# Attention values as 64x64 matmuls without empty columns, and all rounds written out, in a three-attention transformer layer

## The chip, the cores and the metric

The kernel runs on one core of a Trainium2 chip. The metric is the device time of one execution in microseconds. Before the change it is 1069.2 us, the median of three runs (1064.68 to 1073.83). The core has TensorE (PE; its weight loads are PEld), VectorE (DVE), ScalarE (ACT), GpSimd (POOL) and the DMA queue of SyncE (SP). Each runs its own stream of instructions and they wait for each other on semaphores. All data is fp32.

## What is computed

64 sequences of 64 tokens with 256 features go through self-attention (A), cross-attention (B), an MLP (M), and a second cross-attention (C), each with 16 heads of 16 features:

```python
def attention(q, k, v, mask):
    scores = jnp.einsum('bhqd,bhkd->bhqk', q, k) / jnp.sqrt(jnp.float32(HD))
    scores = scores * mask - 10000.0 * (1.0 - mask)
    probs = jax.nn.softmax(scores, axis=-1)
    return jnp.einsum('bhqk,bhkd->bhqd', probs, v)

x = x + merge(attention(A's q, k, v of layernorm(x))) @ w_ao + b_ao
x = x + merge(attention(B's q of layernorm(x); k, v of ctx)) @ w_co + b_co
x = x + gelu(layernorm(x) @ w1 + b1) @ w2 + b2
y = x + tanh(gate) * merge(attention(C's q of x; k, v of layernorm(ctx))) @ Wo.T
```

## The kernel before

**Tiling.** A unit is 4 sequences (256 tokens) as T = 2 tiles of 128 rows; a tile holds TILE = 2 sequences of 64 tokens. There are U = 16 units. Round i works on five units at once: P (load and first statistics) on unit i, A on i-1, B on i-2, M on i-3 and C on i-4. So there are rounds 1 to 19 for TensorE, of which the first and last few work on fewer stages. Rounds 5 to 15 run as a hardware loop (`Fori`, function `run`), the others are written out. Within a round the order of each engine is that of its `body`, written by hand; TensorE's goes: `turn` of C.xT and B.cT, C.K and C.Q, `turn` of M.zT and A.zT, B.V, B.zT, scores C, B.K, B.Q, M.H0, M.H1, scores B, M.H2, attend C, A.K, A.Q, A.V, M.H3, C.OT, M.cT, scores A, C.AO, attend B, M.Y0, B.OT, M.V (values of C for the next round), attend A, B.AO, A.OT, M.Y1, A.AO.

**Banks.** PSUM has 8 banks: `s_bank0` to `s_bank3` for everything of attention, `pj0` to `pj3` for the projections, given out in turn (table PJ); `claim` waits until a bank's last use was read. M.H0 claims the bank that B.V was in, so it waits for `value_rows` of B.

**Attention.** 16 heads are 8 pairs. Bank r = 2t + half holds tile t and 4 pairs. Scores (L482) use 64 rows of the array at a time, the two halves by turns. VectorE masks them into `prob` (`mask_scores`, L847), GpSimd adds the offset (not for C), VectorE takes row maxima (`row_max`, L852), GpSimd subtracts them (L1089), ScalarE takes exp (L692). Then `turn_probs` (L493) transposes each 128x128 block back into the same bank and ScalarE copies it to `prob` (`turned_back`, L698). `values` (L504), for each quarter r, has 4 matmuls with a 128x128 block of transposed probabilities as the stationary operand (the weights: 128 rows are 2 sequences x 64 keys, 128 columns the 64 queries of the pair's two heads) and `vz` as the moving one: 66 columns, for each sequence b2 the 32 values of the pair and a one. In `vz` the rows of the other sequence are zero, so that the sequences stay apart: every column is half empty, and of the results each half of the partitions uses only its own head's 16 of 32 columns. The column of ones gives the sum of the probabilities.

**Reading.** `value_rows` (L841) copies the projection of V into `vz`, by tile and sequence, 4 copies of 64 partitions x 256 elements. `normalise` (L861, L866) takes, for each quarter r, the reciprocal of the sums and multiplies, once for each half of the partitions: 3 instructions, 12 in a unit. `turn_out` (L521) transposes `o` once all quarters are normalised; ScalarE and VectorE make the high and low part of it (`oT_hi` L651, `oT_lo` L828), and the output projection (C.AO and so on, L446) reads both.

An fp32 matmul of the program appears in the trace as two records of MATMUL and two of LDWEIGHTS; a transpose or an fp32r one (the projections) as one of each.

## Time and profile before

| | |
|---|---|
| median of the runs | 1069.2 us |
| span of the profiled execution | 1072.6 us |
| TensorE, weight loads | 967.9 us (90%), 929.0 us (87%) |
| VectorE | 866.5 us (81%) |
| ScalarE, GpSimd | 576.3 us (54%), 561.3 us (52%) |
| mean granted TensorE clock | 0.947 of 2.4 GHz |

Busy time counts an engine's instructions from start to end; matmuls overlap, so a busy TensorE is not one at its peak. The profiled execution is 3.4 us above the median of the runs. Times in rows are microseconds from the start of the span, durations of one instruction nanoseconds where the form says so.

### The profile page before, as it was taken

What the parts mean: (1) busy time and instruction counts of PE and PEld (TensorE: products, weight loads), DVE (VectorE), ACT (ScalarE), POOL (GpSimd) and SP (SyncE); (2) the same over time, 40 slices, a digit from 0 to 9 for tenths busy, and PEclk for the clock granted to TensorE, in tenths of its full rate; (3) what the DMA queues carried; (4) which work ended last, traced back from release to release, by engine and by line L of the source; (5) the groups of instructions that cost most, each with busy time, mean ns of one, the idle gap of its engine ahead of it and who ended that gap; (6) DMA issues with size and microseconds to landing.
All of it is one profiled execution on the core that took longest, in us unless ns stands there. A gap on an engine that the chain in (4) does not pass through costs nothing.

```text
span 1072.6 us, 23111 instructions
## 1 busy us (share of the span) xinstructions
PE 967.9 (90%) x8336; PEld 929.0 (87%) x8336; DVE 866.5 (81%) x1946; ACT 576.3 (54%) x1109; POOL 561.3 (52%) x566
## 2 busy tenths in 40 slices
PE   6977799999999998999999898999999899998876
PEld 6866798989989998988999898998999899998875
DVE  6586979888897978889797988889797888778553
ACT  3444646565474556646464656547455664646342
POOL 2254647457283746638274745728474563727221
PEclk9589999998999899999989999899989999898995
DMA  5030100101000010101001010100101010000000
GB/s 192 0 96 1 36 1 12 37 11 36 11 10 26 9 35 10 35 10 35 10 0 35 10 35 10 35 10 0 35 10 35 10 36 1 26 13 7 17 10 10
DMA packets 32936, 25.74 MB, mean 24 GB/s; under 512 B 12672, under 2 KB 32000, under 8 KB 32896
## 3 DMA queue, kind: packets, MB, share of 16 engines
q1 hardware_dynamic: 32896, 25.20, 7.9%
q8 instruction: 26, 0.43, 0.2%
q14 instruction: 14, 0.11, 0.0%
HBM read 20.99 MB, written 4.19 MB: 23 GB/s over the span
## 4 chain that ended last, share of the span: by engine, by line
PE 44%; DVE 32%; issue 11%; POOL 6%; ACT 6%; DVEq 1%; DMA 0%; ACTq 0%; POOLq 0%; SPq 0%
PE s_bank L504 12%; PE pj L446 10%; PE s_bank L493 7%; PE pj L431 6%; DVE o L866 5%; PE pj L460 4%; DVE rmax_A L852 3%; POOL prob_AC L1089 2%; DVE prob_AC L847 2%; DVE stats L892 2%; DVE z_A L906 2%; PE pj L521 2%; DVE rmax_C L852 2%; PE s_bank L482 2%; DVE z_B L906 2%
## 5 line engine op out<-in xcount | busy, mean ns | idle before, releaser
L683 ACT ACTIVATE k<-pj,kbias,consts 128x256 f32<-128x256 f32 x192 | 92.7, 564 | 143.1 <-PE pj L431 143.1
L1065 POOL TENSOR_TENSOR veps<-mv,eps 128x2 f32<-128x2 f32 x64 | 15.6, 243 | 263.2 <-DVE mv L898 263.2
L1089 POOL TENSOR_TENSOR prob_AC<-prob_AC,rmax_C 128x512 f32<-128x512 f32 x64 | 65.6, 1054 | 125.4 <-DVE rmax_C L852 125.4
L692 ACT ACTIVATE prob_AC<-prob_AC 128x512 f32<-128x512 f32 x128 | 81.1, 636 | 89.5 <-POOL prob_AC L1089 89.4
L1096 POOL TENSOR_TENSOR h_lo<-g,h_hi 128x512 fp32r<-128x512 f32 x64 | 81.4, 1292 | 47.3 <-DVE h_hi L1051 47.3
L482 PE MATMUL s_bank<-k,q 64*128 64x128 f32 x1536 | 100.3, 281 | 6.3 <-ACT q L670 3.8
L482 PEld LDWEIGHTS s_bank<-k,q 64*128 64x128 f32 x1536 | 91.0, 191 | 14.2 <-issue 4.7
L504 PE MATMUL s_bank<-vz_C,prob_AC 128*128 128x66 f32 x512 | 74.7, 316 | 16.5 <-ACT prob_AC L698 16.5
L504 PEld LDWEIGHTS s_bank<-vz_C,prob_AC 128*128 128x128 f32 x512 | 72.7, 231 | 19.5 <-issue 19.4
L1080 POOL TENSOR_TENSOR prob_AC<-prob_AC,maskA_off 128x512 f32<-128x512 f32 x64 | 79.9, 1284 | 17.2 <-DVE prob_AC L847 17.2
L1080 POOL TENSOR_TENSOR prob_B<-prob_B,maskB_off 128x512 f32<-128x512 f32 x64 | 83.0, 1329 | 10.7 <-DVE prob_B L847 10.6
L651 ACT ACTIVATE oT_hi<-pj,bias 128x256 fp32r<-128x256 f32 x96 | 40.0, 470 | 89.2 <-PE pj L521 89.2
L431 PE MATMUL pj<-zT_M_hi,w_hi_M 128*128 128x256 f32 x256 | 75.6, 296 | 6.9 <-DVE vz_B L841 6.9
L698 ACT ACTIVATE prob_AC<-s_bank 128x512 f32<-128x512 f32 x128 | 66.7, 621 | 14.1 <-PE s_bank L493 14.1
L460 PE MATMUL pj<-w_hi_M,h_hi 128*128 128x256 f32 x256 | 74.1, 289 | 0.0
L493 PE MATMUL s_bank<-consts,prob_AC 128*128 128x128 f32 x512 | 67.5, 287 | 6.4 <-ACT prob_AC L692 3.3
L431 PE MATMUL pj<-zT_M_lo,w_hi_M 128*128 128x256 f32 x256 | 72.8, 284 | 0.0
L431 PE MATMUL pj<-zT_M_hi,w_lo_M 128*128 128x256 f32 x256 | 72.7, 284 | 0.0
L460 PE MATMUL pj<-w_lo_M,h_hi 128*128 128x256 f32 x256 | 71.6, 280 | 0.0
L460 PE MATMUL pj<-w_hi_M,h_lo 128*128 128x256 f32 x256 | 71.5, 279 | 0.0
L493 PEld LDWEIGHTS s_bank<-consts,prob_AC 128*128 128x128 f32 x512 | 60.4, 148 | 8.9 <-issue 5.4
L1089 POOL TENSOR_TENSOR prob_AC<-prob_AC,rmax_A 128x512 f32<-128x512 f32 x64 | 65.6, 1049 | 4.2 <-DVE rmax_A L852 3.6
(199 smaller groups left out, 3324.7 us busy)
## 6 DMA issues: line engine op xcount, KB each, us to landing
x_in<-in_x SPq DMA_DIRECT2D x16, 256.0 KB, 2.7
ctx_b<-in_ctx SPq DMA_DIRECT2D x16, 256.0 KB, 2.9
ctx_c<-in_ctx SPq DMA_DIRECT2D x16, 256.0 KB, 2.8
out<-y SPq DMA_DIRECT2D x16, 256.0 KB, 2.2
g<-in_w_M SPq DMA_DIRECT2D x2, 1024.0 KB, 7.1
maskB<-in_mask_Bx1xSxS_ff SPq DMA_DIRECT2D x32, 64.0 KB, 2.6
prob_AC<-in_w_A_qkv SPq DMA_DIRECT2D x1, 768.0 KB, 4.5
prob_B<-in_w_B_kv SPq DMA_DIRECT2D x1, 512.0 KB, 6.1
```

The source lines that it names most:

```text
L431: last = nc.tensor.matmul(bank[:, m * TOK:(m + 1) * TOK], wt[:, k, col + m * P:col + (m + 1) * P], x[:, k, :], start=(n == 0), stop=(n == ...
L446: last = nc.tensor.matmul(bank[:, t * H:(t + 1) * H], x[:, k, t * P:(t + 1) * P], wt[:, k, col:col + H], start=(n == 0), stop=(n == 3 * KC ...
L460: last = nc.tensor.matmul(bank[:, 0:H], x[:, k, t * P:(t + 1) * P], wt[:, k, :], start=(n == 0), stop=(n == 3 * (FF // P) - 1))
L482: mm = nc.tensor.matmul(bank[:, c, :, b2, :], q2[rows_, c, t * TILE + b2].rearrange("p e q -> p (e q)"), k2[rows_, c, t * TILE + b2], star ...
L493: last = nc.tensor.transpose(s_bank[r][:, n * P:(n + 1) * P], prob[a][:, r, n, :], ident[:, :])
L504: last = nc.tensor.matmul(s_bank[r][:, n * TILE * VW:(n + 1) * TILE * VW], prob[a][:, r, n, :], vz[a][:, t, half * BL + n, :, :], start=Tr ...
L683: last = nc.scalar.activation(k2[:, m, :, s, :], k_all[:, m], ACT.Identity, bias=kbias[:, "ABC".index(a), s, m:m + 1], scale=parity[:, 2 + ...
L692: nc.scalar.activation(p2, p2, ACT.Exp).then_inc(exped[a], 1)
L698: nc.scalar.activation(prob[a][:, r, :, :].rearrange("p n k -> p (n k)"), s_bank[r][:, :], ACT.Copy).then_inc(turned_in[a], 1)
L1080: nc.gpsimd.tensor_tensor(p3, p3, of_tile(maskA_off if a == "A" else maskB_off, a, r), ALU.add).then_inc(offset[a], 1)
L1089: nc.gpsimd.tensor_tensor(p3, p3, rmax[a][:, r, :].unsqueeze(2).broadcast_to([P, BL * TILE, S]), ALU.subtract).then_inc(shifted[a], 1)
L1096: nc.gpsimd.tensor_tensor(h_lo[:, 2 * m:2 * m + 2, :], g[:, m, :, :], h_hi[:, 2 * m:2 * m + 2, :].bitcast(F32), ALU.subtract).then_inc(h_l ...
```

## The change

`values` works on squares of 64x64 of the array. For each tile t, pair m, head e of the pair and sequence b2 there is one matmul: the weights are the 64 rows of b2 and the 64 columns of e of the same transposed block, the moving operand is 16 value columns and the one, and the result goes to the partitions of e in bank 2t + b2, columns 17m to 17m + 16. `vz` has no zeros any more (VW is 17), and the results have no unused columns. A unit has 64 matmuls where it had 16. Values of a tile start when both its quarters are turned back, as they write to both banks of the tile. `value_rows` is one copy, `normalise` two instructions for each of two tiles, and the banks are waited for by tile. The four banks are one tensor. `run` writes out all rounds. One more wait (`const_in`) stands ahead of each tile's values; it is long fulfilled.

```diff
-VW = 2 * HD + 1
+VW = HD + 1
...
-            for i in range(first, min(FIRST, last + 1)):
-                body(i)
-            with eng.Fori(FIRST, U) as i:
-                body(i)
-            for i in range(U, last + 1):
+            for i in range(first, last + 1):
                 body(i)
...
-                    read = masked if b[0][0] == "S" else normed
-                    pe.wait_ge(read[b[0][2]], R * (b[1] - 1) + r + 1)
+                    if b[0][0] == "S":
+                        pe.wait_ge(masked[b[0][2]], R * (b[1] - 1) + r + 1)
+                    else:
+                        pe.wait_ge(normed[b[0][2]], T * (b[1] - 1) + r // HALVES + 1)
...
-                pe.wait_ge(turned_in[a], R * u + r + 1)
-                t, half = divmod(r, HALVES)
-                for n in range(BL):
-                    last = nc.tensor.matmul(s_bank[r][:, n * TILE * VW:(n + 1) * TILE * VW],
-                                            prob[a][:, r, n, :], vz[a][:, t, half * BL + n, :, :],
-                                            start=True, stop=True)
-                last.then_inc(summed[a], 1)
+                pe.wait_ge(turned_in[a], R * u + HALVES * (t + 1))
+                pe.wait_ge(const_in, 16)
+                for m in range(NPAIR):
+                    half, n = divmod(m, BL)
+                    for e in range(2):
+                        for b2 in range(TILE):
+                            rows_ = slice(b2 * S, (b2 + 1) * S)
+                            mm = nc.tensor.matmul(
+                                s_banks[e * S:(e + 1) * S, t * HALVES + b2, m * VW:(m + 1) * VW],
+                                prob[a][rows_, t * HALVES + half, n, e * S:(e + 1) * S],
+                                vz[a][rows_, t, e, m, :], start=True, stop=True)
+                            if (m, e) == (NPAIR - 1, 1):
+                                mm.then_inc(summed[a], 1)
...
-                for t in range(T):
-                    for b2 in range(TILE):
-                        rows_ = slice(b2 * S, (b2 + 1) * S)
-                        dst = vz[a][rows_, t, :, b2, 0:2 * HD].rearrange("p m (e f) -> p m e f", e=2)
-                        last = nc.vector.tensor_copy(dst, v[rows_, t])
-                last.then_inc(pj_free[pj_bank(name)], 1)
+                dst = vz[a][:, :, :, :, :].rearrange("p t e m v -> p (t e m) v")[:, :, 0:HD]
+                nc.vector.tensor_copy(dst, pj[pj_bank(name)][:, :].rearrange("p (n f) -> p n f", f=HD)).then_inc(
+                    pj_free[pj_bank(name)], 1)
...
-                for r in rs:
-                    dve.wait_ge(summed[a], R * u + r + 1)
...
+                for t in ts:
+                    dve.wait_ge(summed[a], TILE * (T * u + t + 1))
+                    sums = s_banks[:, t * HALVES:(t + 1) * HALVES, 0:NPAIR * VW].rearrange(
+                        "p b (m v) -> p b m v", v=VW)
+                    nc.vector.reciprocal(rden[a][:, t, :, :], sums[:, :, :, HD]).then_inc(inverted[a], 1)
+                    dve.wait_ge(inverted[a], T * u + t + 1)
+                    nc.vector.tensor_tensor(
+                        o[:, t * TILE:(t + 1) * TILE, :, :], sums[:, :, :, 0:HD],
+                        rden[a][:, t, :, :].unsqueeze(3).broadcast_to([P, TILE, NPAIR, HD]),
+                        ALU.mult).then_inc(normed[a], 1)
...
-                    if active("B", i):
-                        normalise("B", i, [r])
+                    if active("B", i) and r % HALVES == 0:
+                        normalise("B", i, [r // HALVES])
```

TensorE in attend C of a written-out round, before: the transposes of the fourth quarter, then values (each row is followed by what it waits for):

```order
L493 MATMUL s_bank<-consts,prob_AC 128x128 [waits exped_C,masked_B]
L493 MATMUL s_bank<-consts,prob_AC 128x128 x3
L504 MATMUL s_bank<-vz_C,prob_AC 128x66 [waits turned_in_C,pj_free2]
L504 MATMUL s_bank<-vz_C,prob_AC 128x66 x3
L504 MATMUL s_bank<-vz_C,prob_AC 128x66 [waits turned_in_C]
L504 MATMUL s_bank<-vz_C,prob_AC 128x66 x3
```

and the same place after:

```order
L469 MATMUL s_bank<-consts,prob_AC 128x128 [waits exped_C,masked_B]
L469 MATMUL s_bank<-consts,prob_AC 128x128 x3
L485 MATMUL s_bank<-vz_C,prob_AC 64x17 [waits const_in,turned_in_C,pj_free2]
L485 MATMUL s_bank<-vz_C,prob_AC 64x17 x31
L485 MATMUL s_bank<-vz_C,prob_AC 64x17 [waits const_in,turned_in_C]
L485 MATMUL s_bank<-vz_C,prob_AC 64x17 x31
```

Four groups of 4 matmuls, one for each quarter, have become two of 32, one for each tile.

VectorE from `normalise` of C to the low part of C.OT, before (of the four quarters the last):

```order
L861 RECIPROCAL rden_C<-s_bank 128x8 [waits summed_C]
L866 TENSOR_TENSOR o<-s_bank,rden_C 64x2x64 [waits inverted_C]
L866 TENSOR_TENSOR o<-s_bank,rden_C 64x2x64
L841 COPY vz_A<-pj 64x8x32 [waits pj_full3]
L841 COPY vz_A<-pj 64x8x32 x3
L1051 CAST h_hi<-g 128x512 [waits pj_free0,pj_full1]
L828 SCALAR_TENSOR_TENSOR oT_lo<-pj,bias,oT_hi 128x256 [waits hi_C_OT]
```

and after, all of it:

```order
L836 RECIPROCAL rden_C<-s_bank 128x16 [waits summed_C]
L838 TENSOR_TENSOR o<-s_bank,rden_C 128x256 [waits inverted_C]
L836 RECIPROCAL rden_C<-s_bank 128x16 [waits summed_C]
L838 TENSOR_TENSOR o<-s_bank,rden_C 128x256 [waits inverted_C]
L876 TENSOR_SCALAR z_A<-x_in,mv,rstd 128x256 [waits ln_rstd_A]
L876 TENSOR_SCALAR z_A<-x_in,mv,rstd 128x256
L815 COPY vz_A<-pj 128x32x16 [waits pj_full3]
L1021 CAST h_hi<-g 128x512 [waits pj_free0,pj_full1]
L806 SCALAR_TENSOR_TENSOR oT_lo<-pj,bias,oT_hi 128x256 [waits hi_C_OT]
```

Of the 16 instructions for `rden_C`, `o` and `vz_A` that stood ahead of the low part of C.OT, 5 are left; the rest of VectorE's order is the same.

## Rows read from the trace of the kernel before

**Rows 1.** Page: the span, and each engine's busy time, share and instructions.

```profile
span 1072.6 us, 23111 instructions
PE 967.9 (90%) x8336; PEld 929.0 (87%) x8336; DVE 866.5 (81%) x1946; ACT 576.3 (54%) x1109; POOL 561.3 (52%) x566
```

**Rows 2.** Timeline of TensorE, first transposes of five rounds: start, duration (us), instruction.

```profile
156.40 0.60 PE L415 MATMUL pj<-consts,x 128*128 128x128 f32 x4
...
216.89 0.49 PE L415 MATMUL pj<-consts,x 128*128 128x128 f32 x3
...
462.99 0.60 PE L415 MATMUL pj<-consts,x 128*128 128x128 f32 x4
...
523.59 0.60 PE L415 MATMUL pj<-consts,x 128*128 128x128 f32 x4
...
586.06 0.60 PE L415 MATMUL pj<-consts,x 128*128 128x128 f32 x4
```

**Rows 3.** Waits: who waited for whom; us in total, times, longest.

```profile
POOL prob_AC L1089 <- DVE rmax_C L852: 125.4, 18, 17.6
ACT prob_AC L692 <- POOL prob_AC L1089: 89.4, 110, 8.0
...
PE pj L415 <- DVE z_B L906: 20.2, 15, 2.6
...
PE pj L446 <- DVE oT_lo L828: 16.7, 12, 2.4
PE s_bank L504 <- ACT prob_AC L698: 16.5, 14, 1.2
...
PEld pj L521 <- DVE o L866: 8.9, 16, 3.1
...
PE pj L431 <- DVE vz_B L841: 6.9, 14, 0.5
```

**Rows 4.** Stretches: from:to, length; busy (x) by engine; clock, DMA share, GB/s.

```profile
27.10:31.00 3.90, 3.90 (x21) 3.90 (x20) 2.06 (x3) 0.33 (x1) 3.90 (x5) 0.50 0.00 0
35.50:41.70 6.20, 6.20 (x32) 6.20 (x30) 2.35 (x9) 5.07 (x8) 0.00 (x0) 0.50 0.00 0
549.30:556.00 6.70, 6.70 (x33) 6.70 (x33) 6.38 (x17) 1.11 (x3) 6.70 (x8) 0.50 0.00 0
566.00:569.50 3.50, 3.50 (x34) 3.50 (x32) 2.94 (x8) 1.28 (x3) 3.50 (x5) 1.00 0.54 152
```

**Rows 5.** Line L394: durations (ns) min/median/max, first and last start (us), shapes.

```profile
L394 PE MATMUL pj<-consts,prob_B x8: 250/250/272, 24.7 to 25.5; 128*128 128x1 f32 x8
```

**Rows 6.** Timeline of TensorE: start of values B; transposes, scores A, C.AO.

```profile
503.55 0.67 PE L504 MATMUL s_bank<-vz_B,prob_B 128*128 128x66 f32 x5
...
560.01 0.60 PE L415 MATMUL pj<-consts,ctx_c 128*128 128x128 f32 x4
560.54 2.06 PE L482 MATMUL s_bank<-k,q 64*128 64x128 f32 x32
562.53 0.39 PE L446 MATMUL pj<-w_hi_C_o,oT_hi 128*128 128x256 f32 x1
562.75 0.28 PE L446 MATMUL pj<-w_hi_C_o,oT_lo 128*128 128x256 f32 x1
```

**Rows 7.** Timeline of ScalarE: exp of B, and its four turned-back quarters.

```profile
499.44 2.20 ACT L692 ACTIVATE prob_B<-prob_B 128x512 f32<-128x512 f32 x4
502.30 2.06 ACT L698 ACTIVATE prob_B<-s_bank 128x512 f32<-128x512 f32 x4 [0.66 <-PE s_bank L493]
```

**Rows 8.** Groups by line: shapes, count, busy us, mean ns, idle before.

```profile
L847 DVE TENSOR_TENSOR prob_B<-s_bank,maskB 128x512 f32<-128x512 f32 x64 | 39.9, 685 | 2.4 <-PE s_bank L482 2.0
...
L866 DVE TENSOR_TENSOR o<-s_bank,rden_B 64x128 f32<-64x128 f32 x128 | 36.9, 289 | 3.1
...
L841 DVE COPY vz_B<-pj 64x256 f32<-64x256 f32 x64 | 26.8, 419 | 0.6
...
L861 DVE RECIPROCAL rden_B<-s_bank 128x8 f32<-128x8 f32 x64 | 13.3, 208 | 11.0 <-PE s_bank L504 9.0
```

More of the change, by code:

```diff
@@ L194, in build @@
         k2 = sb("k2", [P, KC, UB, 2, S])
-        vz = {a: sb(f"vz_{a}", [P, T, NPAIR, TILE, VW]) for a in "ABC"}
+        vz = {a: sb(f"vz_{a}", [P, T, 2, NPAIR, VW]) for a in "ABC"}
         prob = {"B": sb("prob_B", [P, R, BL, TILE * S]),
@@ L201, in build @@
         rmax = {a: sb(f"rmax_{a}", [P, R, BL * TILE]) for a in "ABC"}
-        rden = {a: sb(f"rden_{a}", [P, R, BL * TILE]) for a in "ABC"}
+        rden = {a: sb(f"rden_{a}", [P, T, TILE, NPAIR]) for a in "ABC"}
         o = sb("o", [P, UB, NPAIR, HD])
@@ L207, in build @@
         h_lo = sb("h_lo", [P, FF // P, TOK], F32R)
-        s_bank = [ps(f"s_bank{r}") for r in range(R)]
+        s_banks = ctx.enter_context(nc.psum_tensor("s_bank", [P, R, BANK], F32))
+        s_bank = [s_banks[:, r, :] for r in range(R)]
         pj = [ps(f"pj{n}") for n in range(PJ_BANKS)]
@@ L479, in scores @@
                                 rows_ = slice(half * S, (half + 1) * S)
-                                bank = s_bank[t * HALVES + half][:, :].rearrange(
+                                bank = s_bank[t * HALVES + half].rearrange(
                                     "p (c s b k) -> p c s b k", c=KC, s=2, b=TILE)
@@ L511, in attend @@
                     turn_probs(a, r, i)
-                for r in range(R):
-                    values(a, r, i)
+                for t in range(T):
+                    values(a, t, i)
             def turn_out(a, i):
                 name = f"{a}.OT"
-                pe.wait_ge(normed[a], R * (unit(a, i) + 1))
+                pe.wait_ge(normed[a], T * (unit(a, i) + 1))
                 bank = claim(name, i)
@@ L772, in _ @@
             for a in "ABC":
-                last = nc.vector.memset(vz[a][:, :, :, :, :], 0.0)
-            last.then_inc(zeroed, 1)
-            dve.wait_ge(zeroed, 1)
-            for a in "ABC":
-                for b2 in range(TILE):
-                    last = nc.vector.memset(vz[a][b2 * S:(b2 + 1) * S, :, :, b2, 2 * HD:VW], 1.0)
+                last = nc.vector.memset(vz[a][:, :, :, :, HD:VW], 1.0)
             last.then_inc(ones_set, 1)
@@ L835, in value_rows @@
                 dve.wait_ge(pj_full[pj_bank(name)], pj_use(name, i))
-                v = pj[pj_bank(name)][:, :].rearrange("p (t e m f) -> p t m e f", t=T, e=2, m=NPAIR)
-                for t in range(T):
-                    for b2 in range(TILE):
-                        rows_ = slice(b2 * S, (b2 + 1) * S)
-                        dst = vz[a][rows_, t, :, b2, 0:2 * HD].rearrange("p m (e f) -> p m e f", e=2)
-                        last = nc.vector.tensor_copy(dst, v[rows_, t])
-                last.then_inc(pj_free[pj_bank(name)], 1)
+                dst = vz[a][:, :, :, :, :].rearrange("p t e m v -> p (t e m) v")[:, :, 0:HD]
+                nc.vector.tensor_copy(dst, pj[pj_bank(name)][:, :].rearrange("p (n f) -> p n f", f=HD)).then_inc(
+                    pj_free[pj_bank(name)], 1)
             def mask_scores(a, r, i):
@@ L853, in row_max, with normalise @@
                                         AX.X, ALU.max).then_inc(maxed[a], 1)
-            def normalise(a, i, rs=range(R)):
+            def normalise(a, i, ts=range(T)):
                 u = unit(a, i)
-                for r in rs:
-                    dve.wait_ge(summed[a], R * u + r + 1)
-                    t, half = divmod(r, HALVES)
-                    sums = s_bank[r][:, 0:BL * TILE * VW].rearrange("p (n v) -> p n v", v=VW)
-                    nc.vector.reciprocal(rden[a][:, r, :], sums[:, :, 2 * HD]).then_inc(inverted[a], 1)
-                    dve.wait_ge(inverted[a], R * u + r + 1)
-                    for e in range(2):
-                        rows_ = slice(e * S, (e + 1) * S)
-                        last = nc.vector.tensor_tensor(
-                            o[rows_, t * TILE:(t + 1) * TILE, half * BL:(half + 1) * BL, :],
-                            sums[rows_, :, e * HD:(e + 1) * HD].rearrange("p (n b) f -> p b n f", b=TILE),
-                            rden[a][rows_, r, :].rearrange("p (n b) -> p b n", b=TILE).unsqueeze(3).broadcast_to(
-                                [S, TILE, BL, HD]), ALU.mult)
-                    last.then_inc(normed[a], 1)
+                for t in ts:
[8 more added lines that the diff above has]
+                        ALU.mult).then_inc(normed[a], 1)
             def tokens_out(stage, bank_use, dst, residual, i):
```

6 lines of the change are left out of this document (3 added, 3 removed).

## The prediction

> **What bounds the kernel now.** The page comes first: TensorE is busy for 90% of the span and its weight loads for 87%, VectorE for 81%, ScalarE and GpSimd for about half [rows 1]. So TensorE carries the time, with VectorE close behind. Next the timeline of TensorE: the start of each round is the first transpose of L415. A straight round took 216.89 - 156.40 = 60.49 us, two rounds of the loop 60.60 and 62.47 us [rows 2]. The view of waits tells what stands in TensorE's way [rows 3]: each round it waits for `z_B` (20.2 us in 15 waits, 1.3 us each), for `vz_B` (0.5 us), for the first turned-back probabilities of C (16.5 in 14, 1.2 us) and, in about every second round, for `oT_lo` (16.7 in 12, 1.4 us); its weight loads wait for `o` (8.9 us in 16; without the longest, 0.4 us each). The table of stretches shows why rounds differ: from 549.3 to 556.0 us, in the values of C that follow that 1.2 us wait and in A.K behind them, the granted clock was 0.5 (1.2 of 2.4 GHz) [rows 4]. A round with this dip is 1.9 us longer; the work lost is more, up to half of these 6.7 us, some 3.1 us, since such a round swallows the wait for `oT_lo` of C.
>
> **The change: the values matmuls.** Now a unit of one attention has 16 matmuls in the program, which the trace shows as 32 pairs of weight load and matmul; they run at 3.5 us for 32 [rows 4], 0.11 us a pair. After, it has 64, so 128 pairs, each with 64 weight columns and 17 moving columns instead of 128 and 66. What sets the pace? The setup matmuls of L394 move a single column against 128 weight columns, and 8 of them start within 0.8 us [rows 5]: again 0.11 us. So the weight columns set it. I take half the columns as half the time, 0.055 us a pair (an estimate; nothing here loads 64 columns). Then how many squares run at once? Scores work on two halves of the array's rows, 128 weight columns each: 32 pairs from 560.54 to 562.53 us, 1.99 us, of which 0.2 is taken off below: 0.056 us a pair [rows 6]: two at a time. The squares differ in row half from one to the next too. Bounds for the 128 pairs:
> - all four squares at once: 128 x 0.055 / 4 = 1.8 us;
> - two at a time: 128 x 0.055 / 2 = 3.5 us;
> - no better than a pair of scores: 128 x 0.056 = 7.2 us.
>
> I take two at a time, which is what the nearest row shows, and 3.5 us, no different from today.
>
> [...] No run here has such small squares.
>
> **Entering and leaving the squares.** Around the scores TensorE loses time: the last of four transposes (560.01 us, 0.11 us apart) would hand over at 560.45, scores start at 560.54; their 16 double steps of 0.11 us would end at 562.32, C.AO starts at 562.53, and its second matmul comes 0.22 us after the first instead of 0.12 [rows 6]. That is 0.4 us for in and out. Values have no such cost now and get it three times a round; in C the way in lies under a wait. [...] So values cost +0.4 us each: +0.3 in C, +0.4 in B and A, **+1.1 us a round**.
>
> **Coarser wait.** Values now start after two turned-back quarters, not one. ScalarE turns them back 0.52 us apart (4 in 2.06 us) [rows 7]. In C, where TensorE waits for the first, this costs 0.5 us. In B the second is back at 502.30 + 1.03 = 503.33, and values start at 503.55 today [rows 6, 7]: hidden, with 0.2 us to spare. If that cover is gone, 0.2 to 0.5 us each. A is alike.
>
> **VectorE.** `value_rows`: 4 copies of 64x256 at 0.42 = 1.68 us become one of 128x512 from PSUM; the like-sized L847 takes 0.69, so -1.0 us. `normalise`: 4 x (0.21 + 2 x 0.29) = 3.15 us become 2 x (0.21 + a 128x256 multiply). That multiply lies between 0.29 and 0.69; I take 0.45: 1.3 us, so -1.85 [rows 8]. Per round -8.5 us of VectorE's work. It is worth only what TensorE waits for:
> - `vz_B` copied 1.0 us sooner ends the 0.5 us wait before M.H0. Behind it row maxima of C, GpSimd's shift, ScalarE's exp and the turning back also come 1.0 us sooner (each waits for the one before, [rows 3]); less the 0.5 for the second quarter, values of C start **0.5 us** sooner. The M.H0 gain is contained in that, as TensorE waits again in C.
> - `oT_lo` of C: VectorE reaches it 2.85 us sooner (normalise C, copy of `vz_A`). In a round without the dip its wait, some 1.3 us, goes; the dipped round has none to lose. But ScalarE's exp of B then bounds: its activations end at 501.6, the turning back begins at 502.3 [rows 7], and TensorE, which came to values of B at 503.55 [rows 6], can gain little more than what exp itself starts sooner by; I keep half, **-0.7**.
> - `o` before B.OT: **-0.3** in all rounds, as `normalise` of B ends sooner.
>
> **Straight code.** Straight and looped rounds differ by 0.1 us [rows 2]: **-0.1**. TensorE's instruction stream grows by half (8336 to some 12,900 matmuls); that it flows 128 pairs in 3.5 us, 27 ns a pair, is not shown by a row. The scores' 56 ns is the nearest, and 7.2 us the bound above.
>
> **Sum.** Round without dip: 1.1 - 0.5 - 0.7 - 0.3 - 0.1 = -0.5. With dip: +0.2. Some 13 full rounds, half and half: about -2 us. The three filling and three draining rounds wait on chains through VectorE: the waits for `o` beyond the steady ones and sooner `vz` are worth 0.5 to 1 us a round, about -4. From its own span of 1072.6 us: 1066.6. The profiled execution is 3.4 us above the median of 1069.2, so in the median's terms **1063 us**.
>
> **Rivals.**
> - *Four squares at once.* For it: scores start their two halves together, so the array runs tiles apart. Against: nothing shows two column halves in the same rows. 1.8 us instead of 3.5, thrice a round, is -5.1; TensorE would then stand longer for exp and z_B, so I keep two thirds, -3.4 x 13 = -44, with the other rounds -50: 1013 us.
> - *The clock.* With one moving column per load the granted clock was 0.5 (27.1 to 31.0 us), and it stayed there through dense values of A (35.5 to 41.7 us), while values of B at full clock kept it [rows 4]. Squares move 17 columns at a time, side by side. If values of B or of A cost a dip in each round and C in each instead of half, that is 13 x 3.1 + 6 x 1.9 = +52; if both B and A do, +92. With 1063: 1115 to 1155. [...] This is the slower side: it decides once one further dip a round appears.
> - *Squares hardly overlap, or the stream of instructions limits.* At 0.04 us a pair, 5.1 us: +1.6 x 48 = +77, 1140; at the bound, +178, 1240.
> - *Faster VectorE buys nothing*: then +1.1 x 16 less 4, 1077, within the same forecast.
>
> **Chances.** Two at a time without further dips 0.35 (own range 1050 to 1078); four at once or close to it 0.27; the clock 0.2; slow squares 0.18. A difference of 1% is about what a measurement can tell. Faster by over 1% (below 1058.5): 0.27 and a third of 0.35 less what the clock eats, 0.37; within 1%: 0.24; slower: 0.39. The range of 1005 to 1130 leaves out the fastest of the second case and the slow tails, each about 0.1.
>
> **What would show it.** The rows of values: 128 pairs in 3.5 us (right), under 2.5 (four at once), over 5 (slow). Granted clock in values of B and A: 1.00, or 0.50. The start of C.AO no longer waiting for `oT_lo`. `normalise` of C in 1.3 us instead of 3.2. VectorE's busy time near 866 - 8.5 x 16 = 730 us. The forecast is wrong above all if 64 weight columns don't load in half the time of 128, or if the column halves of the array run apart.

## The result and the profile after

The changed kernel takes 1011.4 us (median; 999.65 to 1023.91), the kernel before 1069.2 us: a ratio of 0.9395, 95% interval 0.9346 to 0.9445, so 6% faster. The forecast was 1063 us, no change. The profiled execution is the slowest of its runs, 1023.9 us; places and pauses below are read from it, sizes from runs.

The page of the kernel after, answering to [rows 1], with the instruction queues' rows and the shares of the chain that ended last:

```profile
span 1022.1 us, 30512 instructions
PE 913.7 (89%) x12944; PEld 867.1 (85%) x12944; DVE 722.3 (71%) x1412; ACT 571.3 (56%) x1109; POOL 561.7 (55%) x566
...
q8 instruction: 104, 1.70, 0.7%
...
PE 74%; DVE 12%; issue 6%; ACT 4%; POOL 3%; DMA 0%; SPq 0%; DVEq 0%; ACTq 0%; POOLq 0%
```

VectorE has lost 144 us of busy time (forecast: 730 us left). TensorE is the bound. The queue q8, which brings instructions, moved 104 packets of 16 KB; before it was 26.

TensorE in one round with no stop inside values (start, duration, instruction, in brackets the idle time), answering to [rows 2] and [rows 6]:

```profile
738.62 0.60 PE L389 MATMUL pj<-consts,x 128*128 128x128 f32 x4
...
746.04 0.66 PE L389 MATMUL pj<-consts,z_B 128*128 128x128 f32 x4 [0.75 <-DVE z_B L876]
...
761.22 2.06 PE L485 MATMUL s_bank<-vz_C,prob_AC 64*64 64x17 f32 x128 [1.22 <-issue]
763.21 0.38 PE L405 MATMUL pj<-zT_A_hi,w_hi_A_qkv 128*128 128x256 f32 x1
...
772.19 0.39 PE L420 MATMUL pj<-w_hi_C_o,oT_hi 128*128 128x256 f32 x1
772.41 0.28 PE L420 MATMUL pj<-w_hi_C_o,oT_lo 128*128 128x256 f32 x1
...
775.86 2.06 PE L485 MATMUL s_bank<-vz_B,prob_B 64*64 64x17 f32 x128
777.84 0.39 PE L434 MATMUL pj<-w_hi_M,h_hi 128*128 128x256 f32 x1
778.07 0.28 PE L434 MATMUL pj<-w_hi_M,h_lo 128*128 128x256 f32 x1
...
788.52 0.38 PE L420 MATMUL pj<-w_hi_B_o,oT_lo 128*128 128x256 f32 x1 [0.53 <-issue]
...
793.87 0.60 PE L389 MATMUL pj<-consts,x 128*128 128x128 f32 x4
```

The round takes 793.87 - 738.62 = 55.25 us, where it was 60.5. Each values takes 1.98 us from its first square to the next operation (761.22 to 763.21, 775.86 to 777.84), where it was 3.5: three times 1.5 is 4.5 of the 5.2 us. The stand at 788.52, behind values of A, is not in the shortest rounds of this trace: the one from 324.61 us takes 54.42. C.AO no longer waits for `oT_lo`. Values of C still stand 1.2 us, now for the second turned-back quarter.

But only some rounds are like that. TensorE in values of A at 425 us of the same kernel:

```profile
425.31 1.82 PE L485 MATMUL s_bank<-vz_A,prob_AC 64*64 64x17 f32 x111 [0.35 <-issue]
429.09 0.43 PE L485 MATMUL s_bank<-vz_A,prob_AC 64*64 64x17 f32 x17 [1.96 <-issue]
429.44 0.47 PE L420 MATMUL pj<-w_hi_B_o,oT_hi 128*128 128x256 f32 x1
429.71 0.42 PE L420 MATMUL pj<-w_hi_B_o,oT_lo 128*128 128x256 f32 x1
429.93 0.42 PE L420 MATMUL pj<-w_lo_B_o,oT_hi 128*128 128x256 f32 x1
```

After 111 of 128 pairs TensorE stands still for 2 us, with nothing to wait for, and then goes on at half the clock (a matmul of 256 columns every 0.22 us instead of 0.12). The table of stretches (from:to, length; busy time and count of PE, PEld, DVE, ACT, POOL; granted clock; DMA) has it, with the half clock behind the same at 476 us and the round from 738.6 us below:

```profile
427.20:429.10 1.90, 0.01 (x3) 0.01 (x2) 0.03 (x1) 0.00 (x0) 0.00 (x0) 1.00 0.00 0
429.40:432.70 3.30, 3.30 (x23) 3.27 (x18) 0.98 (x3) 0.00 (x0) 0.00 (x0) 0.53 0.03 5
...
479.00:484.10 5.10, 5.10 (x28) 5.08 (x24) 1.28 (x3) 1.89 (x3) 2.07 (x3) 0.50 0.28 73
738.60:793.80 55.20, 52.03 (x806) 49.48 (x805) 44.39 (x86) 34.47 (x68) 34.96 (x36) 1.00 0.09 24
```

This happens in 11 of the 48 values, 1.4 to 2.4 us each, 22 us together. Four more stands of this kind lie behind values, among other matmuls: 2.8 us long at 718.7, 0.8 at 787.7, 1.5 at 818.7 and 1.2 at 837.7 us. The waits of the kernel after, answering to [rows 3] (us in total, times, longest):

```profile
PE s_bank L485 <- issue: 41.6, 39, 2.1
...
PE pj L389 <- DVE z_B L876: 13.2, 15, 2.6
...
PE pj L420 <- DVE oT_lo L806: 7.1, 5, 2.0
```

The wait for `oT_lo` fell from 16.7 to 7.1 us, that for `z_B` from 20.2 to 13.2, that for `vz_B` before M.H0 is gone. What stands in front of squares is now "issue", 41.6 us: the turned-back quarters of C in most rounds, and the stops.

VectorE's new instructions, by shape (ns: least, median, most), answering to [rows 8]:

```profile
L838 DVE TENSOR_TENSOR o<-s_bank,rden_B x32: 423/424/426, 77.3 to 944.1; 128x256 f32<-128x256 f32 x32
...
L836 DVE RECIPROCAL rden_B<-s_bank x32: 245/257/258, 77.0 to 943.8; 128x16 f32<-128x16 f32 x32
...
L815 DVE COPY vz_B<-pj x16: 678/680/681, 55.9 to 919.1; 128x512 f32<-128x512 f32 x16
```

### The profile page after: what moved, and what is told of

The parts are those of the page before. It is cut to its first block, busy times and chain, and to the rows that moved or that the text cites. A ratio compares the mean times of both kernels' runs of the same rounds, so it can differ in the third digit from the quotient of the medians.

```text
span 1022.1 us, 30512 instructions
## 1 busy us (share of the span) xinstructions
PE 913.7 (89%) x12944; PEld 867.1 (85%) x12944; DVE 722.3 (71%) x1412; ACT 571.3 (56%) x1109; POOL 561.7 (55%) x566
## 4 chain that ended last, share of the span: by engine, by line
PE 74%; DVE 12%; issue 6%; ACT 4%; POOL 3%; DMA 0%; SPq 0%; DVEq 0%; ACTq 0%; POOLq 0%
PE pj L405 20%; PE pj L420 13%; PE s_bank L485 10%; PE pj L434 10%; PE s_bank L469 9%; PE s_bank L458 7%; DVE z_B L876 4%; PE pj L389 2%; PE pj L504 2%; DVE stats L862 1%; POOL rstd L1037 1%; DVE h_hi L1021 1%; DVE oT_lo L806 1%; PE pj L368 1%; DVE xT_C_lo L801 1%
## 5 line engine op out<-in xcount | busy, mean ns | idle before, releaser
L675 ACT ACTIVATE prob_AC<-prob_AC 128x512 f32<-128x512 f32 x128 | 77.8, 643 | 75.4 <-POOL prob_AC L1059 75.4
L434 PE MATMUL pj<-w_hi_M,h_hi 128*128 128x256 f32 x256 | 80.2, 313 | 2.7 <-issue 2.7
L434 PE MATMUL pj<-w_hi_M,h_lo 128*128 128x256 f32 x256 | 76.7, 300 | 0.9 <-issue 0.9
L434 PE MATMUL pj<-w_lo_M,h_hi 128*128 128x256 f32 x256 | 76.6, 299 | 0.0
L806 DVE SCALAR_TENSOR_TENSOR oT_lo<-pj,bias,oT_hi 128x256 fp32r<-128x256 f32 x96 | 41.5, 473 | 35.9 <-ACT oT_hi L634 35.9
L1059 POOL TENSOR_TENSOR prob_B<-prob_B,rmax_B 128x512 f32<-128x512 f32 x64 | 66.7, 1071 | 0.0
```

What stands on the lines that cost most here:

```text
L434: last = nc.tensor.matmul(bank[:, 0:H], x[:, k, t * P:(t + 1) * P], wt[:, k, :], start=(n == 0), stop=(n == 3 * (FF // P) - 1))
L675: nc.scalar.activation(p2, p2, ACT.Exp).then_inc(exped[a], 1)
L1059: nc.gpsimd.tensor_tensor(p3, p3, rmax[a][:, r, :].unsqueeze(2).broadcast_to([P, BL * TILE, S]), ALU.subtract).then_inc(shifted[a], 1)
```

## Experiments: straight code or a loop

Theory at this point: four squares run at once, VectorE's shorter work lets TensorE use that, and TensorE's stops inside values come from its instruction stream. Rivals: the straight code brings the gain or makes the stops; VectorE alone brings the gain.

**The changed kernel again** (`after_again`), on one chip with `e1_loop`, `e2_before_straight` and `e6_vector_undone`.

> The changed kernel once more, for a second profile beside the other runs. Theory of the instruction stream (written-out rounds make TensorE fetch its program, and values of a tile pair use it up faster than it comes): in the profile values again stand still for 1.5 to 2.3 us in roughly 10 of 48 units, at multiples of 256 instructions of TensorE's stream, in sum some 20 us, and the time differs from run to run by 1 to 2%. Rival, that these stalls were an accident of one profiled execution: none or one or two here. Time 1000 to 1024 us under both.

1009.6 us, ratio 0.9435 (0.9386 to 0.9484). Ten of the eleven stops are there again, in the same rounds behind the same pair, 0.7 to 2.2 us each and 17 us together; the one of values of B at 476 us is not. So the place is fixed and the length is not.

**A loop again** (`e1_loop`): rounds 5 to 15 as a hardware loop in the changed kernel. For the long fulfilled wait ahead of each tile's values an increment of a semaphore of its own stands.

```diff
-            for i in range(first, last + 1):
+            for i in range(first, min(FIRST, last + 1)):
+                body(i)
+            with eng.Fori(FIRST, U) as i:
+                body(i)
+            for i in range(U, last + 1):
                 body(i)
```

> The changed kernel with rounds 5 to 15 as a hardware loop again, as before the change; a semaphore increment of TensorE stands in place of the wait for the constants ahead of each tile's values. Theory of the instruction stream: in the loop no pauses inside values, fewer dips of the granted clock, so 20 to 30 us less than the changed kernel: 980 to 990 us; the spread between runs falls to below 0.5%. Rival, straight code helps or costs nothing (a straight round was 0.1 us shorter before): same as the changed kernel within 0.5%, 1003 to 1015 us, with the pauses still there, as a loop body of over 1600 TensorE instructions has to be fetched as well.

1009.1 us, ratio 0.9388 (0.9355 to 0.9421): no difference to straight code, and not the 980 to 990 us of my theory. The stops inside values are gone from the loop, as the theory had it; only two are left, in the straight rounds ahead of it. In their place TensorE stands at each of the ten passages from one iteration to the next, for 2.2 to 2.7 us, 23.5 us together, as much as the stops took; behind eight of the ten the clock falls to half (timeline of TensorE, end of one round, start of the next):

```profile
609.86 0.28 PE L425 MATMUL pj<-w_lo_A_o,oT_hi 128*128 128x256 f32 x1
612.13 0.65 PE L394 MATMUL pj<-consts,x 128*128 128x128 f32 x4 [1.99 <-issue]
...
614.02 0.42 PE L410 MATMUL pj<-cT_C_hi,w_hi_C_k 128*128 128x256 f32 x1
```

Its q8 moved 129 packets, spread over the whole loop; in the kernel before there were 26, and none between 271 and 894 us, that is from the second iteration of its loop to the end of the last, and TensorE did not stand at the edge (0.12 us from start to start across it). So the round of the kernel before, 1032 records of TensorE's matmuls and loads, stayed loaded, and the new one, 1608, is fetched anew each time.

**The kernel before, straight** (`e2_before_straight`), the same edit the other way round.

> The kernel before with nothing changed but all rounds written out. Theory of the instruction stream: values with 32 pairs in 3.5 us use the stream 7 times more slowly than squares do, so no pauses inside values, and the time is that of before within 0.5%: 1064 to 1074 us. Rival, straight code is a gain of its own: 0.3 us or more a round in VectorE's chain behind the loop's edge, 1055 to 1065 us. Third: straight code stalls here too, then over 1080 us.

1069.6 us, ratio 0.9981 (0.9956 to 1.0006). Straight code by itself is worth nothing here, and its 68 packets of q8 come without a stop of TensorE.

## Experiments: how many squares run at once

The order of the 32 squares of a tile decides which neighbours there are. In the change, they differ in the row half (b2), then the column half (e). Each of the three kernels is `e1_loop` with the loops of `values` in another order; the work is the same. Each was run twice.

**Only row halves differ** (`e3_rows_apart`):

```diff
-                for m in range(NPAIR):
-                    half, n = divmod(m, BL)
-                    for e in range(2):
+                for e in range(2):
+                    for m in range(NPAIR):
+                        half, n = divmod(m, BL)
                         for b2 in range(TILE):
```

> The looped version with the 64 matmuls of values in another order: all of one column half of the array first, then the other, so that neighbours differ in row half alone. Theory, each square of the array works by itself and a pair takes 0.055 us on its square: two at a time, 128 pairs in 3.6 us instead of 1.85. If TensorE's 1.7 us in 48 values were all on the path, 1009 + 80 us; with VectorE's chain beside it some of that is hidden, 1035 to 1075 us. Rival, the pace is that of the instruction stream (14 ns a pair in any order): 1.85 us again and 1009 us.

**Only column halves differ** (`e4_cols_apart`): b2 outermost, then m, e innermost.

> As the one before, but neighbours differ in column half alone: all pairs of one row half first. Theory, squares are independent in both directions: 3.6 us for 128 pairs, as with rows apart, and the same time. [...]

**One square at a time** (`e5_one_square`): e and b2 outermost, m innermost.

> As before, with all 16 matmuls of a square behind each other, so that neighbours share both halves: theory of independent squares, one at a time, 128 pairs in 7.1 us (0.055 us each, half of the 0.11 us of 128 weight columns), in which only the few at the borders of the squares overlap. TensorE is then the bound by far: 1009 + 48 x 5.3 less what was hidden, 1200 to 1260 us. Rival, TensorE reorders over many instructions and still overlaps squares: below 5 us.

Values of one unit in the timelines of `e1_loop`, of `e3_rows_apart`, of `e4_cols_apart` and of `e5_one_square` (the last one partly at half clock):

```profile
634.79 2.14 PE L490 MATMUL s_bank<-vz_C,prob_AC 64*64 64x17 f32 x128 [1.17 <-issue]
```
```profile
574.49 3.31 PE L490 MATMUL s_bank<-vz_B,prob_B 64*64 64x17 f32 x128 [0.29 <-issue]
```
```profile
579.08 3.31 PE L490 MATMUL s_bank<-vz_B,prob_B 64*64 64x17 f32 x128 [0.29 <-issue]
```
```profile
540.98 8.06 PE L490 MATMUL s_bank<-vz_B,prob_B 64*64 64x17 f32 x128 [0.29 <-issue]
```

From first to last start at full clock: 1.93 us in the loop and 1.85 in straight code with all four squares, 3.10 with two row halves, 3.10 with two column halves, 6.17 with one. So 48 ns for a square alone, 24 with either neighbour, 14.5 with four: my estimate of 55 ns for 64 weight columns was near, but column halves run apart just as row halves do: squares of one row half and two column halves take half the time of squares one after the other, 3.10 us and 6.17.

The times: 1089.5 us (ratio 1.0148, 1.0067 to 1.0228), 1111.2 us (1.035, 1.0261 to 1.044), 1366.0 us (1.2723, 1.2625 to 1.2821), at a mean clock of 0.910, 0.883 and 0.813 where `e1_loop` has 0.933. All three kernels are slower than I expected: the paces came nearly as they should, the times did not. Two at a time costs 48 x 1.2 = 56 us more than four by the pace alone, and 80 in the kernel's time. The clock can make the rest: `e3_rows_apart` spends 198 us at half clock, `e1_loop` 137, which costs at most half of the difference, 30 us (an estimate). `e4_cols_apart` has the pace of `e3_rows_apart` and is 22 us slower, with 263 us at half clock; why its clock stays low for longer no run shows.

`e3_rows_apart` is nearly the world of my forecast, with VectorE's shorter work and two squares at a time, and it is not 1063 but 1089 us. Its ten loop edges take 25 us, which the forecast did not have; without them it would come to about 1064 (an estimate; no straight version of it was run).

## Experiments: what VectorE's shorter work is worth

**All taken back** (`e6_vector_undone`): `e1_loop` with 4 copies in `value_rows`, and 4 reciprocals and 8 multiplies of half the partitions in `normalise`.

```diff
-                    nc.vector.reciprocal(rden[a][:, t, :, :], sums[:, :, :, HD]).then_inc(inverted[a], 1)
...
+                    for b in range(TILE):
+                        nc.vector.reciprocal(rden[a][:, t, b, :], sums[:, b, :, HD]).then_inc(inverted[a], 1)
...
+                        for e in range(2):
+                            rows_ = slice(e * S, (e + 1) * S)
+                            last = nc.vector.tensor_tensor(
+                                o[rows_, t * TILE + b, :, :], sums[rows_, b, :, 0:HD],
```

> The looped version of the changed kernel with VectorE's savings taken back: value rows in 4 copies of 64 partitions, normalise with 4 reciprocals and 8 half-partition multiplies in a unit. Squares stay. Theory A, the gain is TensorE's (1.65 us less in each of 48 values): VectorE's 8.5 us a round are worth less than 1 us a round, so at most 15 us above the looped version. Theory B, VectorE shares the bound and the squares alone would have given little: 35 to 60 us above the looped version, since TensorE then waits for the low part of C, for o and for the copies in every round.

1091.0 us, ratio 1.0174 (1.0139 to 1.0209): the squares without VectorE's part, in a loop, are 17 us slower than the kernel before, and VectorE's part is worth 82 us on top of the squares, more than the 35 to 60 of theory B. It stands 22 us at its ten loop edges, which the kernel before does not; without them it would come to about 1069 (an estimate). So the squares alone are worth little, but that they lose is not shown. Its page, its chain, and one of its waits:

```profile
PE 918.6 (85%) x12944; PEld 869.9 (80%) x12944; DVE 864.5 (80%) x1940; ACT 576.6 (53%) x1109; POOL 562.3 (52%) x566
...
DVE 41%; PE 38%; issue 12%; ACT 4%; POOL 3%; DVEq 1%; DMA 0%; SPq 0%; ACTq 0%; POOLq 0%
```
```profile
PE pj L509 <- DVE o L849: 38.4, 32, 3.9
```

The chain that ended last runs more through VectorE than through TensorE (41% and 38%; with the short work, in `e1_loop`, 9% and 76%), and TensorE stands 1.2 us before two of three `turn_out`, for `o` (38.4 us in 32 times).

**Only normalise taken back** (`e11_normalise_undone`), **only B's copy** (`e12_copies_B`), **only A's and C's copies** (`e13_copies_AC`):

> The looped changed kernel with only normalise taken back to 4 reciprocals and 8 half-partition multiplies a unit; the copy of V's rows stays one instruction. With both taken back it was 1091.0, 81.9 us above the looped kernel's 1009.1. Theory (VectorE is the bound with squares, each us of its work counts): normalise is some 5.6 of 8.5 us a round, so +54 us, 1063 us, with VectorE busy some 810 us. Rival 1 (only what stands ahead of TensorE's wait for o counts, the copies are hidden): all of it, 1085 to 1091. Rival 2 (the sooner copies of V, which start the row maxima of C, carry most): under +30, below 1040 us.

> The looped changed kernel (1009.1 us), with only the copy of B's value rows taken back to 4 copies of 64 partitions. Theory (the place counts: this copy stands ahead of the row maxima of C, on the chain row maxima, GpSimd, exp, turned back, values of C, and ahead of M.H0): about 1 us later each round, and dips of the clock behind the longer wait: +15 to +25 us, 1024 to 1034. Rival (a share like every other us of VectorE's work, a third of the 44 us that all three copies cost on top of normalise): +8 to +15, 1017 to 1024.

> The looped changed kernel (1009.1 us), with only the copies of A's and C's value rows taken back to 4 copies each. Theory (the place counts): the copy of A stands ahead of the low part of C.OT, for which C.AO waits 0.4 us a round, the copy of C ahead of normalise of A, for which A.OT waits; each is partly hidden: +5 to +12 us, 1014 to 1021. Rival (a share of VectorE's work, two thirds of 44): +20 to +30, 1029 to 1039. If each of the two kernels costs nearly nothing and only together with the slower normalise the copies cost 44, the price lies in VectorE's sum and not in a place.

| taken back | time | more than `e1_loop` | VectorE busy |
|---|---|---|---|
| nothing (`e1_loop`) | 1009.1 | | 723.1 |
| copies of A and C | 1012.9 (ratio 0.9414, 0.9356 to 0.9472) | 3.8 | 754.3 |
| copy of B | 1021.3 (0.9527, 0.9497 to 0.9557) | 12.1 | 741.1 |
| normalise | 1046.8 (0.9763, 0.9723 to 0.9802) | 37.6 | 811.9 |
| all | 1091.0 | 81.9 | 864.5 |

Normalise alone costs 37.6 us for 89 of VectorE's time, between the 54 of my theory and the under 30 of its second rival: not each microsecond counts. The 3.8 us of the copies of A and C are not clear of the noise (the intervals of the ratios overlap). All three copies alone sum to 16 us, but on top of the long normalise they cost 44, for 53 us of VectorE's time. Both my rules for them fail: neither their place nor a fixed share gives 16 and 44. The reading that fits is that with a short `normalise` VectorE has slack that swallows most of a copy, and that where it has little left, most of a microsecond of its work is one of the kernel's.

## Experiments: the turned-back probabilities of C

In a clean round the longest wait left is that of values of C. ScalarE (timeline of the kernel after) does three gelus, six activations, ahead of turning back, while the first of the transposed probabilities already stand ready (the transposes run from 758.09 to 760.00 us):

```profile
757.85 2.30 ACT L693 ACTIVATE g<-pj,bias 128x256 f32<-128x256 f32 x6
760.00 2.09 ACT L681 ACTIVATE prob_AC<-s_bank 128x512 f32<-128x512 f32 x4
```

**Two gelus ahead, one behind** (`e7_back_sooner` on `e1_loop`, `e8_straight_back` on the changed kernel):

```diff
-                    for m in range(GELU - 1):
+                    for m in range(GELU - 2):
                         gelus(m, i)
                 if active("C", i):
...
                     turned_back("C", i)
+                if active("M", i):
+                    gelus(GELU - 2, i)
```

> The looped version with ScalarE turning back the probabilities of C ahead of its third gelu instead of behind it, since TensorE waits 1.5 us a round for the second quarter. Theory, this wait is on the path: values of C start 0.8 us sooner, 12 rounds or so, 5 to 10 us off: 1000 to 1004 us. Rival, the gelu is what VectorE waits for next (the high parts stand between the row maxima of B): no gain or a loss of 5 us.

> The changed kernel, straight code, with one edit: ScalarE turns the probabilities of C back ahead of the third gelu, as in the looped kernel where that gave 22 us (1009.1 to 986.5). Theory: the gain is the end of TensorE's 1.5 us wait in values of C and of clock dips behind it, so it comes in straight code too: 1009.6 - 22, about 988 us. The instruction stream of TensorE is unchanged, so its stops of 1.4 to 2.4 us inside values stay, 11 of them, about 20 us together. Rival: in straight code those stops and their dips dominate, and half of the gain is lost: about 1000 us.

986.5 us in the loop, ratio 0.9202 (0.9144 to 0.9259), and 996.1 in straight code, 0.9284 (0.9258 to 0.9311): 23 and 14 us less than their bases. I had expected 1000 to 1004 and 988, with 1000 as the rival's: the first gave more, the second less. The first is the fastest kernel of this study. About 0.7 us a round comes from the wait, the rest from the clock: values of C and then A.K and A.Q behind them in `e1_loop`, and the same in `e7_back_sooner` (table of stretches; the clock is the third column from the end):

```profile
634.79:636.87 2.08, 2.08 (x129) 2.05 (x129) 2.08 (x5) 0.88 (x2) 2.00 (x4) 1.00 0.00 0
636.87:641.32 4.45, 4.45 (x30) 4.45 (x25) 4.38 (x9) 1.85 (x4) 4.45 (x5) 0.62 0.01 4
```
```profile
561.55:563.62 2.07, 2.07 (x129) 2.04 (x129) 2.07 (x4) 1.60 (x4) 1.99 (x4) 1.00 0.03 8
563.62:566.59 2.97, 2.97 (x30) 2.97 (x25) 2.95 (x6) 1.24 (x3) 2.97 (x4) 1.00 0.00 0
```

The wait ahead of values is 1.4 us in the first and 0.7 in the second (first start after the last transpose). Behind the longer one the same 24 matmuls and the first of A.V take 4.45 us at a clock of 0.62, behind the shorter 2.97 at 1.00. That is 0.7 + 1.5 = 2.2 us in this round. But not each round of `e1_loop` is like that: the pause is 1.4 us in all eleven, and the clock falls behind it in six. Here is one where it does not, values of C and the stretch behind them:

```profile
750.63:752.70 2.07, 2.07 (x128) 2.04 (x128) 2.07 (x5) 0.88 (x2) 1.99 (x4) 1.00 0.03 8
752.70:755.70 3.00, 3.00 (x32) 3.00 (x26) 2.93 (x7) 1.26 (x3) 3.00 (x4) 1.00 0.00 0
```

Eleven times 0.7 and six times 1.5 are 17 us, and the eleven rounds take 631.4 us in `e1_loop` and 614.8 in `e7_back_sooner`, 16.6 less; the rest of the gain lies in the filling and draining rounds. Behind the pause of 0.7 us the clock stays in all eleven. In straight code the trace of `e8_straight_back` still has nine stops inside values, 18 us together. What becomes of the other 9 us between the two gains was not followed further.

## Experiments: where the stream of instructions stops

In the trace of the kernel after, each stop inside values lies at one position: if TensorE's recorded instructions are counted from the start, behind number 193 of every 256. 256 of them fill one 16 KB packet of q8 (26,660 instructions, 104 packets). A values has 256 records, so one boundary falls into each; TensorE stops only where the boundary falls late, behind 186 or more of the 256 records; in nine of the eleven cases the boundary before is only 2 to 5 us back. The packets themselves bear it out, by their times in the trace: in each of the eleven stops a packet of q8 starts 2.2 to 3.1 us before TensorE goes on. For the stop that ends at 429.09 us it is the only one of the stretch, and it starts between 426.80 and 426.90 (DMA view of that tenth of a microsecond):

```profile
q8 instruction: 1, 0.02, 59.9%
```

Where a boundary in values passed without a stop, the packet that belongs to it by count had started 5.3 us before or earlier. The four stands behind values have the same sign, 2.4 to 2.6 us.

Two kernels test this. Both are `e8_straight_back` with waits that are long fulfilled added to TensorE's stream, so that a full round has 1792 = 7 x 256 instructions and the boundary stays at its place; they differ only in how many are added once, in the first round that works on C.

```diff
+            def pad(n):
+                for _ in range(2 * n):
+                    pe.wait_ge(const_in, 16)
...
+                if active("C", i) and active("B", i):
+                    pad(SHIFT if starts("C", i) else PAD // 2)
```

PAD is 136, half of it here and half ahead of values of C; two waits make one instruction (TensorE has 28,604 instructions in the trace of `e9_even` and 28,496 in that of `e10_even_late`, 108 fewer for 216 waits fewer). SHIFT is 176 (`e9_even`) or 68 (`e10_even_late`).

> The kernel just before, with waits that are long fulfilled put into TensorE's stream so that a full round has 1792 instructions, 7 times 256, instead of 1656. The boundary of 256 instructions then falls at the same place in each round: after 127 of the 256 records of the values of C, 137 of B, 16 of A. Theory (TensorE stands still when the next 256 instructions are not there, and that is so only where the boundary lies late in a values, because the one before is then only 2 to 5 us back): no stop longer than 0.6 us inside values in rounds 5 to 17, where the kernel before has about 9. The 136 added instructions cost some 0.02 us each, 2.7 us a round, partly under waits: about +1 us a round against 20 us of stops saved, so 980 to 995 us. Rival (the stops have to do with values themselves, the banks or the clock): they stay, about 20 us, and the added instructions make it 1000 us or more.

> The same as the kernel just before, with the same 136 added instructions a round, but 108 fewer once, in the first round that works on C. That alone moves the boundary of 256 instructions to 235 of the 256 records in values of C, 245 in B and 124 in A, in each full round. Theory of the instruction boundary: two stops of about 2.1 us in each of 13 rounds, 26 stops, 55 us, and more dips of the clock behind them: 50 to 70 us slower than the kernel with the even boundary. Rival: no difference between the two, as they do the same work.

1188.5 us (ratio 1.1063, 1.1029 to 1.1097) and 1222.2 us (1.1419, 1.1336 to 1.1502). My price of an added instruction, 0.02 us, came from no run and was far off: 68 in a row take 7.4 us, 0.11 us each, of which 6 us are a pause of TensorE, so neither kernel is of use. But they can be compared, as only the boundary's place differs, and 108 instructions less in the slower one. Values of B in `e9_even`, boundary behind 137 records:

```profile
556.74 2.06 PE L486 MATMUL s_bank<-vz_B,prob_B 64*64 64x17 f32 x128 [0.29 <-issue]
558.72 0.39 PE L435 MATMUL pj<-w_hi_M,h_hi 128*128 128x256 f32 x1
```

and in `e10_even_late`, boundary behind 245, with the stretch of M.Y0 behind it:

```profile
562.11 2.03 PE L486 MATMUL s_bank<-vz_B,prob_B 64*64 64x17 f32 x122 [0.29 <-issue]
565.95 0.40 PE L486 MATMUL s_bank<-vz_B,prob_B 64*64 64x17 f32 x6 [1.81 <-issue]
...
566.20:571.50 5.30, 5.30 (x30) 5.26 (x28) 1.27 (x3) 1.89 (x3) 2.09 (x3) 0.50 0.15 50
```

In `e9_even` no values of rounds 5 to 17 has a stop. The stands are not all gone, though: in each of rounds 5 to 16 TensorE stands for 0.6 to 1.4 us among the matmuls behind values of A, again at a boundary, which comes 2.7 us behind the one before. In `e10_even_late` values of B stop behind pair 122 in all of rounds 5 to 16, nine times for 1.7 to 2.3 us and three times for 0.6 to 0.9, and behind the stop at 564 us M.Y0 runs at half clock, 2.3 us longer. Values of C, whose boundary lies as late, do not stop in these rounds, against what I expected: behind 6 us of pause they run at half clock, and their boundary comes 5.4 us behind the one before, that of B 2.9. In round 4, which has no added waits ahead of values of C, they do stop, 3.6 us behind the boundary before. So the place of the boundary and the time since the last one go with the stop, not the values as such. The rival, no difference, is out: 34 us, where I had expected 50 to 70.

## Why the prediction was wrong

**"Two at a time" for the 128 pairs failed.** It is the step that put the forecast at no change. I took the pace of scores, 0.056 us a pair at two tiles, as a ceiling of two. It was only what two row halves can show: scores use all columns (`64*128` in [rows 6]). The bounds stood right beside it: 1.8 us for four at once, and 1.85 was measured where I had put 3.5. By the rival's sum (3.4 us a round, 50 in all) the forecast would have been 1013 us, and 1011 was measured. That it comes so near is in part luck: that sum has neither the stops of TensorE nor the 82 us that VectorE's shorter work turned out to be worth.

**The weight of 64 columns, half of 128, held.** 48 ns a square alone at 55 estimated.

**Entering and leaving, +0.4 us, is only half read.** Out costs 0.12 us (128 squares would end at 1.86, the next starts at 1.98) and 0.11 in the next matmul (777.84 to 778.07 instead of 0.12). That is 0.23 us; the way in can't be told here from the wait for the turned-back quarter.

**The coarser wait** came as forecast in C (1.2 us again, though the chain is 1 us sooner) and is hidden in B; values of A show 0.35 us ahead of them.

**VectorE's times held, their worth did not.** 1.33 us for a `normalise` (2 x (0.25 + 0.42)), 0.68 for a copy, 722 us busy at 730 forecast. But "it is worth only what TensorE waits for", some 1.5 us a round, is at best true of the kernel as it was; no run has VectorE's shorter work with the old values. With TensorE 4.5 us a round shorter, VectorE is next: `e6_vector_undone` shows 82 us, 5 a round. The terms are not additive: against the kernel before, squares alone are at +17 us, VectorE's work with squares at two a time at +16 (`e3_rows_apart`), both together at -65; each of the three has some 22 to 25 us of loop edges in it. A sum made edge by edge against the waits of before can't show this. One line of the page of the kernel before, which the prediction did not use, points to it, the shares of the chain that ended last:

```profile
PE 44%; DVE 32%; issue 11%; POOL 6%; ACT 6%; DVEq 1%; DMA 0%; ACTq 0%; POOLq 0%; SPq 0%
```

**The straight code, -0.1 us a round, held** for the kernel before (ratio 0.9981). That the longer stream flows was "not shown by a row": on average it did, but with stops of 2 us that I had no term for. The loop has them too, at its edge.

**One rival's sum is wrong.** "Faster VectorE buys nothing" adds its 1.1 x 16 less 4 to the forecast of 1063, which already has VectorE's gains in it; from the 1069 of before it would be 1083. The range covers both.

**Clock dips in values of B and A as such, the slower rival, did not come**: at four squares the clock stays at 1.00 through the round from 738.6 us. The dips came behind pauses, as in [rows 4] (0.53 behind the stop that ends at 429.09 us, 0.50 in M.Y0 behind the one at 476 us), though not behind each. With one or two squares at a time the mean clock does fall, to 0.81, 0.88 and 0.91; how much of that the squares make and how much the pauses was not separated.

## What to carry to other kernels

Where two limits lie close together (TensorE 90%, VectorE 81%), cost an edit against the second limit too: what takes work from both at once can be worth more than the sum of the parts, and each part alone may bring next to nothing (here +17 and +16 us alone against -65 together, some 22 to 25 us of loop edges in each). When rows show a pace only for the arrangement that they use, they bound it from one side; give the arrangement that no row shows its own chance. Look where TensorE stands with nothing to wait for, and count its instructions: here 256 records of squares took 1.85 us, and in 11 of 48 values TensorE stood still for 1.4 to 2.4 us at a boundary of 256. And a pause can cost as much again in the clock behind it: here one of 1.4 us did so in six of eleven rounds, one of 0.7 us in none.

## What the hardware showed that was not expected

- 128 fp32 pairs of 64 weight columns and 17 moving ones took 1.85 us from first to last start at full clock where neighbours differ in row half and column half (`after`; 1.93 in `e1_loop`), 3.10 where they differ in row half alone (`e3_rows_apart`), 3.10 in column half alone (`e4_cols_apart`) and 6.17 where most share both (`e5_one_square`).
- TensorE's instructions came 256 to a 16 KB packet of q8 (`after`: 26,660 instructions, 104 packets). In values they are used at 7 ns each (256 records in 1.85 us), and in 11 of the 48 values of `after` TensorE stood still for 1.4 to 2.4 us behind number 193 of 256, in nine of them with the boundary before only 2 to 5 us back.
- In all five straight traces with squares (`after`, `after_again`, `e8_straight_back`, `e9_even`, `e10_even_late`), no boundary was passed sooner than 2.2 us after the start of its packet, and each stop inside values ended 2.2 to 3.3 us after it.
- The loop body of `before`, 1032 matmul and load records, drew no packet of q8 between 271 and 894 us (26 in the whole run), and TensorE did not stand at its edge (0.12 us from the last matmul of a round to the first transpose of the next, start to start). That of `e1_loop`, 1608 records, drew packets in each iteration (129 in the run), and TensorE stood 2.2 to 2.7 us at each of its ten edges. No body of a size between them was run.
- In `e9_even`, 68 instructions in a row that hold nothing but fulfilled waits (two each) took 7.4 us of TensorE's queue, 0.11 us each.
- Open: what decides when a packet is sent for, and so whether there is a stop. In the kernel after, the boundary before was 1.9 to 4.6 us back in nine of the eleven stops, but 5.4 and 7.9 in the two others; five values of full rounds with a boundary behind 182 to 214 records did not stop, with 4.4 to 6.5 us. The two sets overlap; the packets' starts tell them apart (2.2 to 3.1 us before TensorE goes on, and 5.5 to 6.5), but what sets these starts is not shown.
